# Combining matmuls in four column tiles, and count matmuls in two row tiles with a bank each

## The reference

```
x = x + cross_attention0(layernorm(x), ctx)           # 16 heads of 8, 1601 keys
x = x + routed_ffn0(layernorm(x))                     # 9 experts, top 2
x = x + gathered_attention1(layernorm(x), ctx, idx)   # 64 keys per query, picked by idx
x = x + routed_ffn1(layernorm(x))                     # 8 experts, top 2, and a shared one
```

```
c_sel = c_kv[arange(b)[:, None, None], indices]
attn = softmax(scores, axis=2)            # over the 64 picked keys
out = einsum('bqkh,bqkhd->bqhd', attn, v)
```

## Time and profile before

| | |
|---|---|
| median of 3 runs | 1537.95 us (1526.84 to 1542.74) |
| profiled execution, its own time | 1533.95 us |
| its span, first to last instruction | 1531.8 us |
| TensorE busy | 1395.9 us, 91% |
| VectorE, ScalarE, GpSimd busy | 71%, 52%, 54% |
| mean granted TensorE clock | 0.964 of full speed |

### The profile page before, as it was taken

How to read it: one execution, slowest core, us unless ns; L and a number is a source line. 1 busy time by engine, 2 the same in 40 slices (tenths; PEclk the granted TensorE clock), 3 DMA queues, 4 the chain that set the end, 5 groups by cost and what they waited for, 6 DMA issues and landing times.

```text
span 1531.8 us, 34069 instructions
## 1 busy us (share of the span) xinstructions
PE 1395.9 (91%) x12588; PEld 804.0 (52%) x12588; DVE 1092.1 (71%) x2283; ACT 789.7 (52%) x1200; POOL 828.1 (54%) x1381
## 2 busy tenths in 40 slices
PE   4899799999999999999999999999999999997987
PEld 2244464357533674347743575346843477334845
DVE  4885578866787668877688667876588776865663
ACT  3457337652575426772376524764266723773451
POOL 4356346755566545664457544675456644544462
PEclk8799899999998999999999999999999999997997
DMA  4505310132102330023201421023300331000111
GB/s 111 144 22 150 81 48 12 30 100 66 34 19 49 90 82 2 22 78 86 55 2 34 96 74 36 12 67 79 83 2 23 77 89 26 1 7 28 41 41 45
DMA packets 97654, 82.12 MB, mean 54 GB/s; under 512 B 17658, under 2 KB 90644, under 8 KB 97492
## 3 DMA queue, kind: packets, MB, share of 16 engines
q1 hardware_dynamic: 96916, 78.72, 19.8%
q10 hardware_dynamic: 576, 1.23, 0.3%
HBM read 67.29 MB, written 12.61 MB: 52 GB/s over the span
## 4 chain that ended last, share of the span: by engine, by line
PE 63%; DVE 20%; ACT 5%; POOL 5%; issue 4%; DMA 1%; SPq 0%; ACTq 0%; POOLq 0%; DVEq 0%
PE ob L788 10%; PE um L846 8%; PE ob L863 7%; DVE mx L1259 7%; PE um L847 7%; PE um L773 6%; PE um L758 6%; PE um L736 4%; ACT probs L1054 2%; DVE mx L1376 2%; DVE big L1372 2%; DVE xn L1157 2%; PE um L830 2%; PE um L913 2%; PE um L730 1%
## 5 line engine op out<-in xcount | busy, mean ns | idle before, releaser
L1259 DVE TENSOR_REDUCE mx<-um 128x2 f32<-128x802 f32 (+1 forms) x512 | 501.6, 989 | 177.3 <-PE um L758 173.6
L1054 ACT ACTIVATE probs<-um 128x1024 f32<-128x1024 f32 (+1 forms) x448 | 425.7, 963 | 215.2 <-PE um L773 211.0
L1452 POOL TENSOR_TENSOR hid<-hid,cwb 128x256 f32<-128x256 f32 (+1 forms) x304 | 217.0, 732 | 265.3 <-DVE hid L1271 130.2
L1060 ACT ACTIVATE hid<-um 128x256 f32<-128x256 f32 (+1 forms) x304 | 116.7, 384 | 346.0 <-PE um L847 336.8
L1458 POOL TENSOR_TENSOR big<-iotab,idx_lo 128x512 bf16<-128x512 bf16 x256 | 272.0, 1078 | 28.3 <-PE um L953 20.4
L788 PE MATMUL ob<-probs,vaug 128*9 128x256 f32 (+1 forms) x3328 | 280.6, 386 | 3.2 <-ACT oT L1035 2.7
L758 PE MATMUL um<-kst,qa 64*128 64x401 bf16 (+1 forms) x1024 | 178.4, 347 | 25.3 <-DMA kst<-k_parts 9.8
L773 PE MATMUL um<-big,kst 64*128 64x256 bf16 (+1 forms) x1664 | 171.1, 280 | 14.5 <-DVE mx L1376 4.8
L1271 DVE TENSOR_TENSOR hid<-hid,um 128x256 f32<-128x256 f32 (+1 forms) x304 | 124.4, 414 | 55.8 <-ACT hid L1060 53.0
L846 PE MATMUL um<-xnT,w1T 128*128 128x256 f32 (+1 forms) x400 | 129.3, 406 | 0.0
L863 PE MATMUL ob<-w2T,hid 128*128 128x128 f32 (+1 forms) x800 | 124.2, 280 | 4.6 <-POOL hid L1452 3.7
(11 more groups left out here) (221 smaller groups left out, 2087.9 us busy)
## 6 DMA issues: line engine op xcount, KB each, us to landing
kst<-k_parts SPq DMA_DIRECT2D x360, 50.0 KB
cwb<-cw_rows SPq DMA_DIRECT2D x112, 128.0 KB, 3.4
k_parts<-big SPq DMA_DIRECT2D x72, 128.0 KB, 1.9
ctx_sb<-in_ctx SPq DMA_DIRECT2D x7, 768.0 KB
cwb<-cw_rows SPq DMA_DIRECT2D x48, 96.0 KB, 3.0
k1st<-k_parts SPq DMA_DIRECT2D x96, 32.0 KB
cwb<-cw_rows SPq DMA_DIRECT2D x48, 64.0 KB, 2.7
cwb<-cw_rows SPq DMA_DIRECT2D x16, 112.0 KB, 3.0
```

The lines of the kernel that those rows point to most:

```text
L1054: act.activation(probs[0:kn, k:k + 2, 0:w], own_banks, ACT.Exp).then_inc(f_read, 1)
L1060: act.activation(hid[0:nr, own % NHID, :], quarter[place[ev][0]][0:nr, 0:NQ], ACT.Silu).then_inc(th_ready, 1)
L1259: dve.tensor_reduce(mx[:, p % 2, s, :, j], pair[:, :, 0:w], AX, ALU.max, negate=True).then_inc(u_read, 1)
L1452: pool.tensor_tensor(h, h, cwb[0:nr, k, :], ALU.mult).then_inc(hw_ready, 1)
```

## The change

Two places of TensorE's work are cut into tiles of the array; `EV` is the same list.

- `combine`: each matmul with 128 stationary columns becomes four with 32 columns, which write partitions 0, 32, 64 and 96 onward (`tile_position=(0, QD * t)`, `QD` is 32). Work and result are the same; a combine has 8 fp32 matmuls in place of 2, so 16 weight loads and 16 matmuls in place of 4 and 4.
- `cnt`: each count matmul becomes two, one for each token of the pair: 64 partitions of `onehot` against the two columns of `idx_c` that belong to these. The two write different banks (`own[0]`, `own[1]`). A step has 16 matmuls in place of 8, the stationary operand of each is 64 x 128, and the step now needs an adjacent pair of banks.
- VectorE's copy reads the same 32 numbers of a partition out of two banks in place of one.
- As `cnt` needs two banks, the walk over `EV` gives other banks to many steps behind it, and so other waits.

```
-  "aT1": 1, "o1": 1, ... "q0": 1, "c0": 1, "cnt": 1, "q1": 1, "c1": 1}
+  "aT1": 1, "o1": 1, ... "q0": 1, "c0": 1, "cnt": 2, "q1": 1, "c1": 1}
...
             def combine(bank, o):
                 for s in range(NS):
-                    m = pe.matmul(bank[:, s * 2 * V1:(s + 1) * 2 * V1], o[:, s * P:(s + 1) * P], comb[:, :], start=True, stop=True)
+                    for t in range(P // QD):
+                        m = pe.matmul(bank[QD * t:QD * (t + 1), s * 2 * V1:(s + 1) * 2 * V1], o[:, s * P + QD * t:s * P + QD * (t + 1)],
+                                      comb[:, :], start=True, stop=True, tile_position=(0, QD * t))
                 return m
...
                 elif kind == "cnt":
-                    cnt = free_bank(ev)[:, 0:QW * NS * KC1].rearrange("p (q n) -> p q n", n=NS * KC1)
+                    free_bank(ev)
+                    own = [quarter[k] for k in place[ev]]
                     pe.wait_ge(onehot_ready, NCNT * b + n + 1)
                     for q in range(QW):
-                        m = pe.matmul(cnt[:, q, :], onehot[:, n % 2, q, :], idx_c[:, QW * n + q, :], start=True, stop=True)
+                        for s in range(NS):
+                            o = NIDX * s
+                            m = pe.matmul(own[s][:, KC1 * q:KC1 * (q + 1)], onehot[o:o + NIDX, n % 2, q, :],
+                                          idx_c[o:o + NIDX, QW * n + q, KC1 * s:KC1 * (s + 1)], start=True, stop=True)
                     m.then_inc(m_psum, 1)
...
                 elif kind == "cnt":
                     dve.tensor_copy(cntT[b % 2].rearrange("p c (s q) -> p q s c", s=NS)[:, QW * n:QW * (n + 1), :, :],
-                                    bank[:, 0:QW * NS * KC1].rearrange("p (q s c) -> p q s c", s=NS, c=KC1)).then_inc(u_read, 1)
+                                    pair[:, :, 0:QW * KC1].rearrange("p s (q c) -> p q s c", c=KC1)).then_inc(u_read, 1)
```

More of the change, by code:

```diff
@@ L301, in build @@
         M_NEED = {"part": 2, "pair1": 2, "xT4": 1, "pq0": 1, "mq": 1, "aT0": 1, "o0": 1, "xT1": 1, "gate0": 1, "xT2": 1, "pq1": 1,
-                  "aT1": 1, "o1": 1, "xT3": 1, "gate1": 1, "ct0": 1, "ct1": 1, "std": 1, "q0": 1, "c0": 1, "cnt": 1, "q1": 1, "c1": 1}
+                  "aT1": 1, "o1": 1, "xT3": 1, "gate1": 1, "ct0": 1, "ct1": 1, "std": 1, "q0": 1, "c0": 1, "cnt": 2, "q1": 1, "c1": 1}
         SERIAL = ("key", "n4a", "n1a", "n2a", "n3a", "le0", "le1")
```

## The result

The changed kernel takes 1546.16 us (median of 20 runs, 1540.78 to 1554.39) against 1533.21 for the kernel before (20 runs, 1523.28 to 1542.74): ratio 1.0088, 95% interval 1.0066 to 1.0109, or 13 us more. The forecast was 1528. (The forecast had leaned towards 1537.95, the median of three runs of before; with twenty runs it is 1533.21.) The profiled execution of after took 1544.56 us.

A forecast was written before the change was run, and what follows sets the result against it. TensorE, busy for 91% of the span, was taken to bound the kernel. 1533.95 less 37 arriving plus 29 of new waits gave 1526, forecast as 1528 us; own range 1511 to 1543, range with rivals 1492 to 1558.

The forecast's parts named there:

- The combining work: TensorE's combine: column tiles overlap, 0.45 to 0.14 us each, saving 39.7 us over 128 combines.
- the two rivals about tiles: TensorE's small matmuls: a 25 ns floor in any tile (1574 us, chance 0.09), or combine tiles don't overlap (1554, 0.05).
- TensorE's total: TensorE's time falls by 46 us: 39.7 from combining plus 9.2 from mode changes less 3 for counts.
- New waits: Bank table: 139 bank waits now late, 43 us summed, 32 after merging near sites, 29 net of lost waits.
- Mode changes: TensorE, array tile shape: 102 fewer changes at 0.09 us each save 9.2 us, all from the count part.
- What of it arrives: Steps behind combines: bank-wait slack lets 31 of the combine's 39.7 us through, so 46 becomes 37.
- the sign of this: TensorE less busy but VectorE's chain share grown as much: gain lost to VectorE in stretches without room.
- the one that the prediction gave 0.09: Rival on count steps' second bank: 43 us of waits undiminished, tiles overlapping only half, 1556 us; chance 0.09.
- my own theory: Written for the follow-up runs: the fuller VectorE is, the less the combine's tiles bring, under 0.5% with a slower comparison.
- The rival that VectorE has room: Follow-up rival on VectorE's comparison: added work costs little, ratio below 1.007; no chance given.
- the one by which slack swallows the same part of either sign: Follow-up rival: slack behind a combine swallows two thirds of any change; doubled combines cost 20 us, ratio 1.010 to 1.017.
- rival F: Follow-up rival: every combine, early or late, brings the same quarter to third of its 0.31 us; no chance given.

The follow-up runs named there:

- bank_only: Kernel before with only the bank-table number for a count step raised from 1 to 2, second bank unused; ratio to before 1.0201, 31 us.
- cnt_only: Kernel before with only the count matmuls in two row tiles and two banks, old combine; ratio to before 1.0245.
- comb_bank: Kernel before with the new combine and two banks for a count step, count matmuls as before; ratio to before 1.0108.
- comb_only: Kernel before with only the new combine in four column tiles, counts as before with one bank; 1522.11 us, ratio to before 0.9911.
- comb_early: Kernel before with column tiles in 104 combines, all but the 24 late ones of the first attention; 1518.95 us, ratio to before 0.9906.
- comb_light: Kernel before with the new combine and VectorE's comparison with zero cut to 8 of 1024 columns; ratio to before 0.9844.
- before_light: Kernel before with VectorE's comparison with zero cut to 8 of 1024 columns, old combine; ratio to before 0.9983.
- comb_eq_slow: Kernel before with the new combine and VectorE's comparison walking all 1024 columns in a slowly read order; ratio to before 1.128.
- comb_eq_mid: Kernel before with the new combine and 256 of the comparison's 1024 columns in slow order; 1562.7 us, ratio to before 1.0161.
- eq_mid: Kernel before with 256 of the comparison's 1024 columns in slow order, in their own instruction, old combine; 1592.49 us, ratio to before 1.0363.
- comb_twice: Kernel before with each of the 128 combines computed twice into the same place; ratio to before 1.0402, 62 us.
- comb_late: Kernel before with column tiles only in the 24 combines of the first attention's last three head pairs; ratio to before 1.0002.

## Why the prediction was wrong

**Where it was right.** The combining work (0.45 to 0.14 us forecast, 0.12 to 0.15 measured, nothing lost to the tiles), the two rivals about tiles (both excluded: a combine reaches the next group in 0.25 us, mode change included, not 0.4), and the copy from two banks. TensorE's total looks right at -47.7 us against -46, but by luck: some 11 of it are the missing records, and like for like it is -36.9. The Trainium skill's page "TensorEngine Tiling (Array Packing)", section "Performance Considerations", gives each matmul about 60 cycles of overhead; if all sixteen of a combine paid it one after the other, that would be an estimated 0.4 us by the page's figure. Here the trace disagrees with this reading: sixteen matmuls in four tiles take 0.25 us, mode change included.

**New waits: the kind right, the size near, in part by luck.** Forecast 32 us (29 net), measured 31 by bank_only. The place shown above waits as long as was read out. The sum as a scale is less good: halving the late releases took 0.4% from bank_only and 0.8% from the whole change, where half of the cost would be 1.0%. How much of the 31 us is the late releases that were added up, and how much follows from other banks in another way, stays open.

**Mode changes: shorter in place, not in time.** 9.2 us less 3 were to come from the count tiles. The single change costs what was forecast: a `part` step with a count step behind it reached it in 0.28 us before and in 0.18 after, where the shape is now the same. cnt_only lies at 1.0245 and bank_only at 1.0201, the whole change 0.2% below comb_bank: together no gain that can be told from none. The count step itself is as short as forecast (sixteen matmuls in 0.20 to 0.22 us to a group of the same shape). That it stands among bank waits, where TensorE waits longer for what it saves, would explain this; it is a reading and not shown.

**"What of it arrives" is the step that failed.** It let 31 of the combine's 39.7 us through, by counting only bank waits within four steps behind a combine. Measured: 14. The prediction itself named the sign of this: TensorE less busy, and VectorE's share of the chain grown by as much. It came half: TensorE's share fell by 11 points and VectorE's rose by 5. With 31 us of waits and 14 that arrive, the case is the one that the prediction gave 0.09, in which the waits exceed what arrives; but not by its mechanism, as the tiles do overlap. Two things were left out; the first is borne out in part, the second is argued.

The first is that VectorE has little room where 104 of the 128 combines stand. The prediction took its load from the batch's average (134.9 of 179) and wrote of 44 us of room. By stretches, in the trace of before (us; busy PE, PEld, DVE, ACT, POOL, each with its count; clock; DMA share; GB/s):

```profile
583.00:603.00 20.00, 17.84 (x207) 8.29 (x206) 18.00 (x35) 14.29 (x18) 11.92 (x21) 1.00 0.01 2
603.00:623.00 20.00, 18.91 (x230) 7.87 (x228) 17.04 (x29) 14.18 (x18) 9.91 (x19) 1.00 0.01 2
623.00:643.00 20.00, 18.74 (x218) 7.83 (x216) 17.73 (x29) 14.39 (x20) 15.88 (x25) 1.00 0.13 41
643.00:663.00 20.00, 17.56 (x204) 7.37 (x200) 17.03 (x33) 13.36 (x19) 14.44 (x27) 1.00 0.08 23
...
720.00:760.00 40.00, 39.90 (x245) 31.87 (x243) 24.70 (x43) 11.21 (x26) 19.35 (x33) 1.00 0.33 77
```

In the first 80 us (583 to 663) VectorE is busy for 69.8 and TensorE for 73.1; most of the room is in the FFN's stretch, behind them (at the end of the table VectorE is busy for 62%). The chain over these 80 us, by line, in before and then in comb_only for the same work (573 to 653; L1261 there is L1259 here, L1378 is L1376, L1374 is L1372):

```profile
by line: PE ob L788 16.4%; PE um L773 10.9%; DVE mx L1259 10.6%; PE um L758 6.2%; PE um L736 6.1%; issue 5.6%; DVE mx L1376 4.5%; PE um L913 4.0%; ACT probs L1054 3.9%; DVE big L1372 3.5%; DVE xn L1157 3.1%; PE um L830 2.8%; PE um L730 2.7%
```

```profile
by line: DVE mx L1261 14.0%; PE ob L790 10.9%; DVE mx L1378 8.5%; PE um L775 8.3%; DVE big L1374 8.0%; issue 7.1%; PE um L760 5.3%; ACT big L1133 3.7%; PE um L915 2.7%; DVE xn L1159 2.5%; PE um L730 2.4%; DVE big L1305 2.3%; PE um L955 1.8%
```

The maximum L1259 rose from 10.6 to 14.0%, that of the second attention from 4.5 to 8.5%, and VectorE's step L1372 from 3.5 to 8.0%: the work that was taken from TensorE left VectorE as what is waited for. The doses say how far this goes (us; in brackets the 95% interval):

| | dose | time |
|---|---|---|
| TensorE, combines | -39.7 us | -14 us (-19 to -8) |
| TensorE, early combines | -32 | -14 (-20 to -9) |
| TensorE, combines | +57.6 | +62 (55 to 68), up to 14 of it clock |
| TensorE, late combines | -7.4 | 0 (-5 to +5) |
| TensorE, late combines | +10.8 | +10 (5 to 15) |
| VectorE, comparison | -32 | -3 (-7 to +2) |
| VectorE, comparison | +67 | +56 (49 to 63), up to 34 of it clock |
| both | -39.7, -32 | -24 (-30 to -17) |

On TensorE added work counts nearly whole and removed work for a third to under a half. On VectorE removed work counts for next to nothing, and added work for a third at least, for most if the clock is left out of account. That is how two engines look that set the pace together, and the difference between the signs is clear of noise for the combines as a whole. It is not for the late ones alone, nor is it shown that more arrives when work is taken from both (the sum of the two alone would be 17). The same page of the Trainium skill, under "PSUM Bottleneck", says that tiling makes TensorE quicker but not the emptying of PSUM, which may then become the bottleneck; the trace agrees, as the maxima that grew in the chain are VectorE's reads of PSUM.

The second is the queue wait at the down matmul: 10.5 us in comb_only's profile, 7.0 in comb_bank's, 1.8 in the whole change's, none in comb_early's. Without it the tiles would have brought some 24 us in comb_only and 28 in comb_light (an estimate: 14 and 21 us, and the 10.5 and 6.9 us by which this row grew in their profiles against before and before_light). This is argued and not shown, and one run speaks against it: comb_early has no such wait, and its 104 combines of 128 still brought 14 us, where by the estimate 19 would be due, at the edge of its interval. The one repair that was tried lost more elsewhere.

**What fell of my own theory.** In its sharp form, that the fuller VectorE is the less the tiles bring, it predicted 0 to 0.5% in comb_eq_slow and comb_eq_mid, and 2.9% and 1.9% came. What stands is that both engines are bounds at the balance that the kernel has; how the gain divides when one of them is loaded is not proportional to its busy share. The rival that VectorE has room fell by eq_mid, even with the clock counted off; comb_twice against comb_only excludes the one by which slack swallows the same part of either sign.

**What stays open.** Whether the late combines bring nothing or the 2 us of rival F, as comb_late's 12 runs spread by 23 us. Its profiled execution, the shortest of the twelve, has the stretch behind them about a microsecond shorter in five of six batches; one batch of six lost 3.8 us in that very stretch. Further, how the 26 us that don't arrive divide between VectorE and the queue, and how much of eq_mid's loss and of comb_eq_mid's gain is clock.

**The sum with the measured sizes:** 1533 - 14 + 31 - 3 (count tiles, from comb_bank to the whole change) = 1547, where 1546 was measured. It shows that the parts add up, not why each has its size.

## What to carry to other kernels

Read the busy shares by stretch, not by period: where a second engine is as full as the bound one (here within 5%), expect only a part of what you remove, here a third, and most of what you add to the bound one. Compare busy times only after counting the records: 58 that were missing here looked like 11 us of saved work. A PSUM bank that a step takes without need costs waits at places far from it, here 2% for one number in a table; write out which reads the new table waits for before timing it. And ask of a speed-up which DMA queue it will arrive at early.

## What was unexpected of the hardware

Sixteen pairs of fp32 load and matmul with 32 columns, four in each of four tiles, fit in 0.12 to 0.15 us; four pairs of 128 columns took 0.45. Count matmuls of 64 rows in two halves of the array take 25 to 28 ns for two, as long as one of 128 rows took, so the second half cost next to nothing here.

VectorE's comparison of 1024 bf16 columns took 0.576 us on the mean when it walked in order, and this when each step jumps by 128 columns:

```profile
L1303 DVE TENSOR_SCALAR big<-big 128x1024 bf16<-128x1024 bf16 x128 | 336.4, 2628 | 14.7 <-POOL big L1458 14.6
```

That is 2.6 ns a column, 4.6 times as long, and GpSimd's step L1458 ahead of it took 1293 ns in that kernel where it takes 1078 in before. The Trainium skill, page "SBUF — State Buffer", section "Door 1: The DMA port swizzle", says that each access which crosses to a new 16-byte line pays a penalty. The trace agrees in so far as the walk with jumps of 256 bytes costs about 2 ns more a column; no run tries another stride, so that the lines are the reason is not shown.

The store `k_parts<-big` of 64 KB took 5.34 us in one kernel and 10.48 in another that differs only in TensorE's matmuls: that the other transfers which it meets had moved may be the reason, but is not shown.
